# Who loads the tokens of later chunks, and when decay rows are loaded, in an attention and expert kernel on one core

## The reference

```python
xn = _layernorm(x, axis=-1)
# attention on xn
S = jnp.einsum('hid,hjd->hij', K, Q) * SCALE
decay = jnp.where(delta < 0, 0.0, -delta.astype(jnp.float32) ** ALPHA)
S = jnp.where(delta < 0, -jnp.inf, S) + decay
C = jax.nn.softmax(S, axis=-1)
attn = jnp.einsum('hij,hjd->hid', C, V)      # then @ o_w.T + o_b  -> s
# experts on xn: top 2 of softmax(x @ gate_w), gelu(x @ fc1 + b1) @ fc2 + b2, weighted -> g = silu(...)
x = x + s * g
```

## Time and profile before

| | us |
|---|---|
| median of 3 runs (719.65 to 725.21) | 722.7 |
| profiled execution, time | 723.35 |
| profiled execution, span | 721.5 |
| TensorE busy | 682.4 |
| VectorE busy | 535.4 |
| ScalarE busy | 485.1 |
| GpSimd busy | 231.4 |

### The profile page before, as it was taken

One profiled execution on the slowest core, in us unless ns is written; L12 is line 12 of the kernel. 1 busy time (PEld: TensorE's weight loads), 2 busy tenths in 40 slices (PEclk: granted clock), 3 DMA queues, 4 the chain that ended last, 5 costly groups with the idle time before them and its releaser, 6 DMA issues.

```text
span 721.5 us, 17539 instructions
## 1 busy us (share of the span) xinstructions
PE 682.4 (95%) x6042; PEld 462.0 (64%) x6042; DVE 535.4 (74%) x1146; ACT 485.1 (67%) x994; POOL 231.4 (32%) x330
## 2 busy tenths in 40 slices
PE   6976999999999999999999999999789999999976
PEld 3865776565555556556555655654359888999764
DVE  6535987999989989998998999896224554444298
ACT  3542443677777877788787777878776666666374
POOL 5331110134023323423342432300034757576300
PEclk9997999899999999999999999999999999999998
DMA  6999966333765685487568657710359686865396
GB/s 194 267 251 308 350 215 198 96 57 74 127 128 138 140 178 148 120 173 159 137 139 171 142 141 149 169 25 19 94 132 251 244 206 216 223 189 177 112 401 245
DMA packets 77207, 124.46 MB, mean 172 GB/s; under 512 B 14184, under 2 KB 47464, under 8 KB 77000
## 3 DMA queue, kind: packets, MB, share of 16 engines
q1 hardware_dynamic: 68368, 98.32, 54.4%
q0 software_dynamic: 8752, 25.02, 10.8%
HBM read 72.56 MB, written 49.72 MB: 169 GB/s over the span
## 4 chain that ended last, share of the span: by engine, by line
PE 82%; DVE 8%; DMA 6%; ACT 2%; issue 2%; POOL 1%; SPq 0%; DVEq 0%; POOLq 0%; ACTq 0%
PE ps L1578 20%; PE ps L1511 14%; PE ps L1562 13%; PE ps L1667 8%; PE ps L1689 8%; PE ps L1500 7%; PE ps L1460 5%; PE ps L1470 3%; DMA arena<-in_x 2%; DMA arena<-xs_dram 2%; PE ps L1650 2%; DVE mxa L1103 2%; DVE arena L1412 1%; DVE x_room L1417 1%; DVE arena L1402 1%
## 5 line engine op out<-in xcount | busy, mean ns | idle before, releaser
L1103 DVE TENSOR_REDUCE mxa<-ps 128x1 f32<-128x512 f32 (+3 forms) x608 | 357.9, 653 | 35.2 <-PE ps L1500 20.3
L967 ACT ACTIVATE arena<-ps 128x512 f32<-128x512 f32 x576 | 304.0, 603 | 82.3 <-PE ps L1562 41.1
L1511 PE MATMUL ps<-aug 57*128 57x512 f32 (+3 forms) x768 | 218.4, 401 | 2.1 <-DVE mxa L1103 0.3
L1562 PE MATMUL ps<-aug 59*128 59x512 f32 (+3 forms) x768 | 216.0, 399 | 0.5 <-ACT arena L967 0.5
L1578 PE MATMUL ps<-arena,v_q 128*32 128x512 f32 (+3 forms) x1536 | 154.9, 498 | 6.7 <-ACT arena L967 6.3
L1562 PEld LDWEIGHTS ps<-aug 59*128 59x128 f32 x768 | 109.9, 186 | 76.2 <-ACT arena L967 69.0
L1511 PEld LDWEIGHTS ps<-aug 57*128 57x128 f32 x768 | 109.6, 186 | 37.2 <-DVE mxa L1103 23.4
L889 POOL DMA_INDIRECT y_dram<-arena,y_row_of x71 | 69.4, 978 | 54.2 <-DVE y_row_of L1341 47.3
L862 POOL DMA_INDIRECT xs_dram<-arena,slot x64 | 62.6, 978 | 74.1 <-ACT arena L967 70.5
L1500 PE MATMUL ps<-key_mask,key_rows 64*128 64x64 bf16 (+2 forms) x704 | 79.0, 208 | 0.0
L1667 PE MATMUL ps<-arena 128*128 128x128 f32 x568 | 75.2, 275 | 0.0
(11 more groups left out here) (148 smaller groups left out, 639.3 us busy)
## 6 DMA issues: line engine op xcount, KB each, us to landing
aug<-k_parts SPq DMA_DIRECT2D x96, 128.0 KB
aug<-q_parts SPq DMA_DIRECT2D x96, 128.0 KB
arena<-xs_dram SPq DMA_DIRECT2D x71, 128.5 KB, 2.6
k_parts<-arena SPq DMA_DIRECT2D x16, 512.0 KB, 5.9
q_parts<-arena SPq DMA_DIRECT2D x16, 512.0 KB, 5.9
arena<-y_dram SPq DMA_DIRECT2D x16, 512.0 KB, 6.7
xn_dram<-arena SPq DMA_DIRECT2D x8, 512.0 KB, 6.9
a_dram<-arena SPq DMA_DIRECT2D x128, 32.0 KB
```

Of the source, the lines that this page charges most:

```text
L967: nc.scalar.activation(prob_slot(q, i), score_bank(q, i), ACT.Exp).then_inc(exp_done, 1)
L1103: nc.vector.tensor_reduce(dst, src, AX.X, ALU.max).then_inc(piece_used, 1)
L1511: ins = nc.tensor.matmul(banks[:, at_ * width:(at_ + 1) * width], k_aug[n][rows, hp, ib * P:(ib + 1) * P], q_aug[n][rows, hp, lo:lo + widt ...
L1562: ins = nc.tensor.matmul(out_[:, col0:col0 + hi - lo], q_aug[n][rows, h // SIDES_OF_ARRAY, jb * P:(jb + 1) * P], k_aug[n][rows, h // SIDES ...
```

## The change

- The loads of chunks 2 to 7 move from SP's queue to GpSimd's. Chunk 2 is loaded when chunk 0 is normalised; chunk i + 2 right behind GpSimd's normalisation of chunk i, after a wait for its own last instruction. Chunk 1 stays with SP, with a semaphore of its own.
- The decay rows of buffer 0 are still loaded behind chunk 1; those of buffer 1 behind chunk 4 (was 2), those of buffer 2 behind chunk 6 (was 3), each behind that step's token load.
- Each buffer's decay rows have their own semaphore. TensorE waited for all three before the first piece; now it waits for a buffer's at the first piece of its quad.

```diff
+DECAYS_AT = (1, 4, 6)
@@ SP
-            def load_x_chunk(b, c):
-                sp.dma_start(xb[c], x_t[:, bass.ds(TB * b + CT * c, CT), :]).then_inc(x_in[c], 16)
-            load_x_chunk(0, 1)
+            sp.dma_start(xb[1], x_t[:, CT:CHUNKS * CT, :]).then_inc(x_second, 16)
-                    if n == 0 and more > 2:
-                        sp.wait_ge(xn_ready, i + 2)
-                        load_x_chunk(b + c + 1, 1 - c)
             sp.wait_ge(xn_ready, 1)
             sp.wait_ge(xn_half, 1)
-            load_x_chunk(1, 0)
             store_normalised(0, 0, 0)
@@ GpSimd
+            def load_x_chunk(i):
+                b, c = i // CHUNKS, i % CHUNKS
+                pool.dma_start(xb[c], x_t[:, TB * b + CT * c:TB * b + CT * (c + 1), :]).then_inc(x_in[c], 16)
+
+            pool.wait_ge(xn_ready, 1)
+            pool.wait_ge(xn_half, 1)
+            load_x_chunk(CHUNKS)
...
                 ins.then_inc(xn_ready, 1)
-                if i <= AUG:
-                    load_decays(i - 1)
+                if i + CHUNKS < CHUNKS * B:
+                    pool.wait_ge(xn_ready, i + 1)
+                    load_x_chunk(i + CHUNKS)
+                if i in DECAYS_AT:
+                    load_decays(DECAYS_AT.index(i))
@@ VectorE, statistics
-                dve.wait_ge(x_in[c], 16 * b + 16)
+                if i == 1:
+                    dve.wait_ge(x_second, 16)
+                elif i > 1:
+                    dve.wait_ge(x_in[c], 16 * b)
@@ TensorE
                         pe.wait_ge(aug_in[(n + d) % AUG], 192 * ((q + d) // AUG) + 192)
+                        if q + d < AUG:
+                            pe.wait_ge(decays_in[q + d], 16 * 2 * SIDES_OF_ARRAY)
...
-                            pe.wait_ge(decays_in, 16 * 2 * SIDES_OF_ARRAY * AUG)
```

More of the change, by code:

```diff
@@ L167 @@
 TRANSPOSE_AT = (1, 2)
+DECAYS_AT = (1, 4, 6)
+assert len(DECAYS_AT) == AUG
 WARMING = 16
@@ L416, in rows_of @@
             return slice(ROW_TILE * side, ROW_TILE * side + count)
-        ident_in = sem("ident_in"); key_in = sem("key_in"); x_half = [sem(f"x_half{n}") for n in range(2)]; xn_half = sem("xn_half"); weights_in = sem("weights_in"); consts_in = sem("consts_in")
+        ident_in = sem("ident_in"); key_in = sem("key_in"); x_second = sem("x_second"); x_half = [sem(f"x_half{n}") for n in range(2)]; xn_half = sem("xn_half"); weights_in = sem("weights_in"); consts_in = sem("consts_in")
         bias_ready = sem("bias_ready")
@@ L424, in attention_moe_kernel @@
         weights_high = sem("weights_high"); wk_low = sem("wk_low"); weights_low = sem("weights_low"); xT_low = sem("xT_low"); xpose_done = sem("xpose_done"); xT_ready = sem("xT_ready")
-        proj_done = sem("proj_done"); first_done = sem("first_done"); proj_out = sem("proj_out"); masks_clear = sem("masks_clear"); masks_set = sem("masks_set"); decays_in = sem("decays_in")
+        proj_done = sem("proj_done"); first_done = sem("first_done"); proj_out = sem("proj_out"); masks_clear = sem("masks_clear"); masks_set = sem("masks_set"); decays_in = [sem(f"decays_in{n}") for n in range(AUG)]
         parts_out = [sem(f"parts_out{c}") for c in range(CHUNKS)]
@@ L505, in _ @@
                 sp.dma_start(xb[0][:, HALF * n:HALF * (n + 1), :], x_t[:, HALF * n:HALF * (n + 1), :]).then_inc(x_half[n], 16)
-            sp.sem_inc(x_in[0], 16)
             sp.dma_start(idf[:, :], ident_f).then_inc(ident_in, 16)
@@ L741, in load_decays @@
                     row = ROW_TILE * side + DATA_ROWS
-                    pool.dma_start(k_aug[n][row:row + DECAY_ROWS, :, :], k_rows[:, 0:HP, :]).then_inc(decays_in, 16)
+                    pool.dma_start(k_aug[n][row:row + DECAY_ROWS, :, :], k_rows[:, 0:HP, :]).then_inc(decays_in[n], 16)
                     pool.dma_start(q_aug[n][row:row + DECAY_ROWS + NSPLIT, :, :], q_rows[:, 0:HP, :]
-                                   ).then_inc(decays_in, 16)
+                                   ).then_inc(decays_in[n], 16)
             for i in range(1, CHUNKS * B):
```

## The result

The changed kernel takes 718.34 us (median of 20 runs, 713.9 to 724.24) where the kernel before takes 724.12 (20 runs, 719.28 to 728.57): the ratio is 0.993, interval 0.9906 to 0.9953. That is 5.8 us by the medians and 5.1 by the ratio, 3.4 to 6.8 by its interval, and under the 1% that the prediction took as what can be told; the interval lies clear of 1. Ratios leave out runs over 1.5% above the fastest of their kernel (one of the kernel before, in a later series, took 1509.55 us). The profiled execution took 721.25 us, span 719.4, so 2.1 us less than the profiled one of before.

A forecast was written before the change was run, and what follows sets the result against it. TensorE's 12.55 us stall in chunks 2 and 3 was all to win; with chunk 2's store and the row loads late next, 3.5 us remained: 723.35 to 719.85 us, 719.2 for a median; own range 716 to 722, whole range 712.5 to 725.

The forecast's parts named there:

- What bounds, and who held the load: TensorE's stall in chunks 2 and 3, 12.55 us; SP's own order, not GpSimd, held chunk 5's load 11.2 us.
- The two coincidences of the trace: Chain puts GpSimd's normalisation ahead of chunk 5's load; chunk 2's last store lands half a microsecond before ScalarE starts chunk 4.
- What is late next: ScalarE's start of chunk 4 waits for chunk 2's last store, landing at 66.3, between 64.2 and 71.1.
- the hole: DMA gap left by the last, narrow decay loads ahead of SP's release, share 0.22 at 46; 1 us taken.
- its 3.9: Most that SP's release could come sooner, if the hole closes fully; 2.3 us was the forecast.
- my sum: DMA work from SP's wait to chunk 2's last store: 18.5 us plus 2.9 before; the change adds 1.3.
- The first piece: TensorE's first piece in chunk 4: quad 0's row loads land near 60, so it waits 5 us.
- quarter step ahead: TensorE has sent chunk 4's second projection when ScalarE starts, formerly only the first: 3.5 us ahead of a 13.90 step.
- The size: Whole kernel: 3.5 us won, 719.2 us for a median execution; chance 0.55.
- the first rival: Chunk 2's stores don't bind, the whole 12.55 us stall goes: 711 to 713 us; chance 0.17.
- The second, nothing: Store lands at 68 to 69, gap as long as before: 722 to 724 us; chance 0.18.
- The third, slower: Chunk 2's last store lands at 71.1, behind GpSimd's loads: up to 2.5 us lost, 726 us; chance 0.10.

The follow-up runs named there:

- the version with a better order on SP: Kernel before with decay rows moved and SP issuing chunk 4's tokens ahead of the constants, chunk 5's ahead of its wait for stores: ratio 0.9956.
- the other two profiles: The changed kernel run again without an edit, in two later series: ratios to the kernel before 0.9912 and 0.9957.
- both later edits: Changed kernel with quad 0's row loads behind chunk 2's stores and the first piece six half steps later (SKIP 22 for 16): ratio 0.9836.

## Why the prediction was right

*What bounds, and who held the load.* Right. The load of chunk 5 leaves 12.4 us sooner (1.5 of them because chunk 3 was normalised at 35.9 and not 37.3), its wait is gone, and it was SP's order: the version with a better order on SP does as well. The two coincidences of the trace (the chain put GpSimd ahead of the load; the store half a microsecond behind it) were read rightly.

*What is late next.* Right in kind and in place: ScalarE's start of chunk 4 at 66.3, forecast for a store that lands between 64.2 and 71.1; measured 66.23, and 60.64 and 63.15 in the other two profiles. SP's release was forecast for 43.6; it came at 44.23, 41.26 and 41.87. The lower bounds were too high, by 0.7 us for the release (42.0) and by 3.6 for the store; with the terms that the prediction names (2.6 for the decay rows, 1.0 for the hole) the release could come 3.6 us sooner, and it doesn't say where its 3.9 comes from. Taking the decay rows away alone released SP 4.8 us sooner, at 41.05. So they may weigh more than the 1.3 us a set that I took, but the release of one kernel moved by 3 us between profiles (by 0.6 between the two of before), and these profiles can't settle it. From the release to ScalarE's start of chunk 4 it took 22.0, 19.4 and 21.3 us in the changed kernel and 21.9 and 19.0 in the one before. No change of that stretch stands out from this spread; my sum had it 1.3 us longer.

*The first piece.* Mis-sized in the profile after: TensorE was to wait 5 us for row loads, it waited 9.06, then 0 and 4.52. My own terms give more than the "near 60" that I wrote. From the measured release, 44.23 + 2.9 for start and landing (I had put 1.2) + 12 row loads + 1.3 each for the store between them, chunk 6's tokens and the decay rows is 63.0, and the first piece came at 62.97. So in that execution TensorE was not the quarter step ahead that I gave it: its second projection of chunk 4 began at 67.52, after ScalarE's start. In the second profile it began at 57.73, ahead of ScalarE's start at 60.64; in the third at 62.80, about with it (63.15).

*The size.* Forecast 3.5 us, measured 5.8 by the medians and 5.1 by the ratio (3.4 to 6.8). That the number came this near is in part luck. The sum took SP's release at 43.6, a store at 66.3 and a quarter step ahead. In the one profile near those times (44.23 and 66.23) the quarter step wasn't there and nothing was won; in the other two release and store came earlier than forecast. The wait at the first piece was put too short in the first and the store too late in the others, and the two errors offset each other. What I called the first rival, the full 12.55 us, fell: no profile has ScalarE start chunk 4 before 60, though 60.64 is near it. The second, nothing, describes the first pair of profiles (within 0.1 us of nothing, net of the clock at the start) and not the medians. The third, slower, didn't occur; the version with row loads behind the stores gave the whole gain back (1.0003), but by a wait for row loads, not by the store that this rival named.

*The rest.* GpSimd's issue took 0.79 to 0.94 us, as its nearest row said, and no wait for chunk 2's load or for later decay rows is in the trace. The wait of GpSimd for the stores of normalised tokens, which I had held to be in time, is there: 15.1 us until 63.91 at chunk 5, 2.3 us ahead of ScalarE's start and not the 4 that I gave it. It did no harm there, since TensorE's transposes of those tokens, at 70.63, wait for nothing. By the rule of the Trainium skill, "DMA: Bandwidth & Descriptors", section "Issuing engines are not separate DMA queues", another issuer saves only issue time; the trial with the order on SP agrees (0.9956 against 0.9957). The starvation that the Trainium skill, "SBUF — State Buffer", section "SBUF: two separate sides", warns of isn't seen: no issue of tokens took over 0.94 us, and the loads of chunks 4, 5 and 6 landed 6.2, 7.1 and 8.3 us after their issue, where SP's load of chunk 5 took 8.5. Whether VectorE ran such a mode there no run shows.

## What to carry to other kernels

Before taking a stall for the gain, look for what lands just behind it. Here a store landed half a microsecond before ScalarE started the next chunk, and when the 9 us wait for tokens went, that store and 12 row loads held the same work. In this stretch, with the DMA engines full, moving one transfer forward moved the wait to the next one. Two things can help then: to take out of the stretch ahead of a barrier what nothing needs yet (the decay rows; alone 0.9967, with an interval that reaches 1), and to put the work that needs the late data later (0.9888 with the first piece six half steps later). Neither is a rule: with the stores first as well, starting the pieces three half steps earlier or later than that gave 0.9949 and 0.9932. And take several profiles before sizing a gain of under 1%.

## What the runs showed of the hardware

The same instruction sequence reached its DMA-bound points at different times: SP's release at 41.26, 41.87 and 44.23 us, TensorE's gap at its first piece 0, 4.52 and 9.06 us. What makes the transfers of one execution slower than those of another stays open. The gap of 9.06 us cost more than itself: in it the granted clock went from 1.00 (55 to 56 us) to 0.50 (58 to 59), and behind it six products took 2.74 us instead of 1.55; in the execution with no gap over 1.3 us it stayed at the upper level (50 to 62 us, granted clock 1.00). Gaps of nearly one length went both ways: after 2.74 us with the tokens alone the clock was 0.50 and the next six products of values took 1.69 us, after 2.81 us with both later edits it was 1.00 and they took 0.97.
